# Two-layer graph network on one core: the query and key columns move into the tile of the folded matrices

## The reference

```python
# layer 0
h = relu(layernorm(x));  x = x + adj @ (h @ W0) + b0
# layer 1, 8 heads, n = 128 nodes, dim = 256
h  = relu(layernorm(x))
f  = (h @ fc_w + fc_b)  -> heads x n x 256
q, k = f @ q_w + q_b, f @ k_w + k_b
a  = softmax(leaky_relu(q + k.T + (1 - adj) * -1e9))
x  = x + sigmoid(concat(a @ f) @ fp_w + fp_b + h)
```

## Time and profile before

| | |
|---|---|
| median of 3 runs | 1406.65 us (1406.38 to 1407.17) |
| the profiled execution | 1406.65 us |
| its span, first to last instruction | 1404.9 us |
| granted TensorE clock | 1.0 throughout |
| PE busy | 1394.7 us (99%), 9048 matmuls |
| DVE busy | 1285.1 us (91%) |
| ACT busy | 1126.5 us (80%) |
| POOL busy | 1102.0 us (78%) |

### The profile page before, as it was taken

The page is one execution under the profiler, slowest core; times in us unless marked ns, Lnnn a source line. Parts: engine busy times, 40 slices in busy tenths (PEclk is TensorE's granted clock), DMA queues, the critical chain, the costliest instruction groups (busy, mean ns, idle before and its releaser), DMA issues.

```text
span 1404.9 us, 31603 instructions
## 1 busy us (share of the span) xinstructions
PE 1394.7 (99%) x9048; PEld 1252.5 (89%) x9048; DVE 1285.1 (91%) x4408; ACT 1126.5 (80%) x3429; POOL 1102.0 (78%) x1295
## 2 busy tenths in 40 slices
PE   9999999999999999999999999999999999999998
PEld 7898899899899889998998898998989989988987
DVE  7999999999999999999999999999999999998996
ACT  4878788788888888887888888888878878887876
POOL 4788878878778878778787788787787887888764
PEclk9999999999999999999999999999999999999999
DMA  7423323323223233233232232232332322322221
GB/s 238 98 63 107 107 54 106 91 69 106 71 88 106 55 105 106 54 105 97 63 106 80 79 106 61 99 106 54 105 103 58 106 88 73 106 67 85 77 61 41
DMA packets 177132, 124.69 MB, mean 89 GB/s; under 512 B 137808, under 2 KB 143568, under 8 KB 177104
## 3 DMA queue, kind: packets, MB, share of 16 engines
q1 hardware_dynamic: 176816, 124.35, 30.3%
q10 hardware_dynamic: 288, 0.01, 0.0%
HBM read 105.98 MB, written 18.35 MB: 89 GB/s over the span
## 4 chain that ended last, share of the span: by engine, by line
PE 94%; POOL 2%; issue 1%; DVE 1%; DMA 1%; ACT 0%; POOLq 0%; SPq 0%; ACTq 0%; DVEq 0%
PE gbank L381 48%; PE ybank L381 24%; PE tbank L481 8%; PE bank L381 6%; PE bank L426 4%; PE bank L462 2%; PE bank L449 2%; DMA late<-key_rows 0%; POOL att L1561 0%; POOL att L1554 0%; DMA qk<-qk_w_dram 0%; DVE att L829 0%; POOL xb L1544 0%; POOL t_pos L1546 0%; POOL ends L1577 0%
## 5 line engine op out<-in xcount | busy, mean ns | idle before, releaser
L1233 ACT ACTIVATE att<-att 128x128 f32<-128x128 f32 x1024 | 397.8, 393 | 47.0 <-DVE att L836 44.0
L381 PE MATMUL gbank<-m_hi,hT_lo 128*128 128x512 f32 x1024 | 426.7, 417 | 0.0
L1554 POOL TENSOR_TENSOR att<-late,t_pos 128x512 f32<-128x512 f32 x256 | 330.6, 1293 | 120.5 <-PE tbank L481 115.8
L381 PE MATMUL gbank<-m_hi,hT_hi 128*128 128x512 f32 x1024 | 403.2, 394 | 0.0
L381 PE MATMUL gbank<-m_lo,hT_hi 128*128 128x512 f32 x1024 | 401.3, 392 | 0.0
L812 DVE TENSOR_TENSOR g_lo<-gbank,g_hi 128x512 fp32r<-128x512 f32 x512 | 341.4, 678 | 47.1 <-ACT g_hi L1226 42.0
L1561 POOL TENSOR_TENSOR att<-att,rinv 128x512 f32<-128x512 f32 x256 | 289.4, 1131 | 107.1 <-DVE rinv L841 106.5
L1226 ACT ACTIVATE g_hi<-gbank 128x512 fp32r<-128x512 f32 x512 | 291.1, 595 | 39.6 <-PE gbank L381 39.4
L829 DVE TENSOR_SCALAR_CACHE_REDUCE att<-att,qs 128x128 f32<-128x128 f32 x1024 | 291.6, 341 | 27.0 <-POOL att L1554 26.7
L381 PE MATMUL ybank<-g_hi,pT_hi 128*128 128x256 f32 x1016 | 281.5, 277 | 0.0
L381 PE MATMUL ybank<-g_hi,pT_lo 128*128 128x256 f32 x1016 | 281.4, 277 | 0.0
(11 more groups left out here) (97 smaller groups left out, 2323.1 us busy)
## 6 DMA issues: line engine op xcount, KB each, us to landing
late<-key_rows SPq DMA_DIRECT2D x64, 1024.0 KB, 6.1
g_in<-graph_dram SPq DMA_DIRECT2D x64, 512.0 KB, 3.4
out_dram<-ends SPq DMA_DIRECT2D x63, 256.0 KB, 3.9
qs<-key_rows SPq DMA_DIRECT2D x128, 4.0 KB, 2.5
key_rows<-kq_sb SPq DMA_DIRECT2D x64, 24.0 KB, 1.4
att<-fc_wT_dram SPq DMA_DIRECT2D x4, 256.0 KB, 5.6
late<-fp_w_dram SPq DMA_DIRECT2D x4, 256.0 KB, 5.3
ends<-fp_w_dram SPq DMA_DIRECT2D x2, 512.0 KB, 7.9
```

The source lines that it names most:

```text
L381: mm = pe.matmul(out_ap, w, m, start=first and n == 0, stop=last and n == len(terms) - 1)
L1233: e = act.activation(a[:, s], a[:, s], ACT.Exp, scale=-1.0, bias=a[:, CH + h:CH + h + 1], accum_out=esum[j][c][:, h:h + 1])
L1554: gp.tensor_tensor(a, keys[q][:, j, c * HC:(c + 1) * HC, :], t_pos[q][:, j, :].unsqueeze(1).broadcast_to([P, HC, P]), ALU.add)\
```

## The change

The two query and key columns of each fold no longer go to `u` one fold at a time. They stay next to the matrix they came with, in `m_hi` and `m_lo`, so that one instruction on each of ACT and DVE takes all 258 columns; at the end four small copies on each engine gather all of them into `u`.

- `m_hi` and `m_lo` become `[P, DT, 4, 576]`: for each pair of heads a row of 576 columns, the two matrices at columns 16 to 527, the even head's two extra columns at 14 and 15 and the odd head's at 528 and 529. Their alignment is 256 bytes; a row has 2304 bytes, nine times 256. Each of the two tiles grows from 16384 to 18432 bytes. So the matrices begin at 64 modulo 256, as before. The tiles declared behind begin 4288 bytes later: `g`, `u` and `ident` begin at 0 modulo 256.
- In `fp_sb` the weights lie in rows of 260 columns, with query and key columns on both sides; an even head's fold streams columns 0 to 257, an odd one's 2 to 259. POOL fills both sides in four copies of half the size. PE's `fold` waits for one of them at n = 0, for two at n = 2, for four at n = 8.
- `fold_high` and `fold_low` are one instruction each. `u_high` (ACT, four copies, behind `hT_high(0, 0)`) and `u_low` (DVE, four products with -1, ahead of `hT_low(0, 0)`) are new; the first `queries_keys` waits for these. `u_none` moves from in front of `fold_high(0)` to behind `fold_high(9)`.

```diff
-        m_hi, m_lo = sb("m_hi", [P, DT, H * D], F32R, LINE), sb("m_lo", [P, DT, H * D], F32R, LINE)
+        m_hi, m_lo = sb("m_hi", [P, DT, HP, MROW], F32R, SPAN), sb("m_lo", [P, DT, HP, MROW], F32R, SPAN)
...
+        def u_of(m, dt, k):
+            s = MAT - 2 if k == 0 else MAT + 2 * D
+            return m[:, dt, :, s:s + 2].rearrange("p a k -> p k a").bitcast(F32)
+
+        def fold_at(m, dt, h):
+            s = MAT - 2 if h % 2 == 0 else MAT + D
+            return m[:, dt, h // 2, s:s + D + 2]
...
-                if n == 0:
-                    pe.wait_ge(g_qk, 2)
+                if n in (0, DT, HP * DT):
+                    pe.wait_ge(g_qk, (1, 2, 4)[(0, DT, HP * DT).index(n)])
+                cols = slice(0, D + 2) if h % 2 == 0 else slice(2, D + 4)
...
-                dve.wait_ge(a_uhi, n + 1)
-                dve.scalar_tensor_tensor(out=u_at(dt, h, HALF), in0=gbank[n % RSIZE][:, D:D + 2], scalar=-1.0,
-                                         in1=u_at(dt, h, 0).bitcast(F32), op0=ALU.mult, op1=ALU.subtract)\
-                   .then_inc(v_ulo, 1)
-                s = slice(h * D, (h + 1) * D)
-                dve.tensor_tensor(m_lo[:, dt, s], gbank[n % RSIZE][:, 0:D], m_hi[:, dt, s].bitcast(F32), ALU.subtract).then_inc(v_m, 1)
+                dve.tensor_tensor(fold_at(m_lo, dt, h), gbank[n % RSIZE][:, 0:D + 2], fold_at(m_hi, dt, h).bitcast(F32),
+                                  ALU.subtract).then_inc(v_m, 1)
...
+            def u_low():
+                dve.wait_ge(v_m, H * DT)
+                dve.wait_ge(a_none, 1)
+                for dt in range(DT):
+                    for k in range(2):
+                        dve.tensor_scalar(u_at(dt, HALF, k), u_of(m_lo, dt, k), -1.0, None, ALU.mult).then_inc(v_ulo, 1)
...
                 fold_low(15)
+                u_low()
                 hT_low(0, 0)
...
-                act.activation(m_hi[:, dt, h * D:(h + 1) * D], gbank[n % RSIZE][:, 0:D], ACT.Copy).then_inc(a_m, 1)
-                if n == 0:
-                    act.wait_ge(a_none, 1)
-                act.activation(u_at(dt, h, 0), gbank[n % RSIZE][:, D:D + 2], ACT.Copy, scale=-1.0).then_inc(a_uhi, 1)
+                act.activation(fold_at(m_hi, dt, h), gbank[n % RSIZE][:, 0:D + 2], ACT.Copy).then_inc(a_m, 1)
...
+            def u_high():
+                act.wait_ge(a_m, H * DT)
+                act.wait_ge(a_none, 1)
+                for dt in range(DT):
+                    for k in range(2):
+                        act.activation(u_at(dt, 0, k), u_of(m_hi, dt, k), ACT.Copy, scale=-1.0).then_inc(a_uhi, 1)
...
                 hT_high(0, 0)
+                u_high()
                 h0_relu(2, 2)
...
-                    gp.tensor_copy(w[:, :, D:D + 2].rearrange("p (h t) k -> p h t k", t=DT),
-                                   qk[:].unsqueeze(1).broadcast_to([P, H // 2, DT, 2])).then_inc(g_qk, 1)
+                    for s in (0, 1):
+                        cols = w[:, :, s * (D + 2):s * (D + 2) + 2].rearrange("p (a s t) k -> p a s t k", s=2, t=DT)
+                        gp.tensor_copy(cols[:, :, s], qk[:].unsqueeze(1).broadcast_to([P, HP // 2, DT, 2]))\
+                          .then_inc(g_qk, 1)
```

More of the change, by code:

```diff
@@ L30 @@
 SPAN = 256
+HP = H // 2
+MAT = LINE // 4
+MROW = 2 * D + 64
+FROW = D + 4
 U = 3
@@ L119, in gnn_pair @@
         key_rows = [nc.dram_tensor(f"key_rows{k}", [2 * HALF, P], F32).ap() for k in range(U)]
-        late = sb("late", [P, U * KEYS * P + H * DT])
+        late = sb("late", [P, U * KEYS * P + H * 4])
         keys = [late[:, k * KEYS * P:(k + 1) * KEYS * P].rearrange("p (j h n) -> p j h n", j=J, h=H) for k in range(U)]
@@ L126, in gnn_pair @@
         rinv = [two(f"rinv{j}", [P, HC]) for j in range(J)]
-        ends = sb("ends", [P, 4 * J * D + H * DT])
+        ends = sb("ends", [P, 4 * J * D + H * 4])
         y, th, sg, res = [ends[:, k * J * D:(k + 1) * J * D].rearrange("p (j d) -> p j d", j=J) for k in range(4)]
@@ L135, in gnn_pair @@
         fcT_sb = [w.rearrange("p (t d) -> p t d", d=D) for w in (att_all[:, 0:H * D], late[:, 0:H * D])]
-        fp_sb = [w.rearrange("p (t d) -> p t d", d=D + 2)
+        fp_sb = [w.rearrange("p (t d) -> p t d", d=FROW)
                  for w in (late[:, (U - 1) * KEYS * P:], ends)]
@@ L183, in adjT_of, with u_at @@
             return g_in[q][:, J * D + J * P:].rearrange("p (j n) -> p j n", j=J)
-        def u_at(dt, h, at):
-            return u[:, dt, at:at + ROWS].rearrange("p (k h) -> p h k", k=2)[:, h, :]
+        def u_at(dt, at, k):
+            return u[:, dt, at:at + ROWS].rearrange("p (k a s) -> p k a s", k=2, s=2)[:, :, :, k]
+        def u_of(m, dt, k):
[4 more added lines that the diff above has]
+            return m[:, dt, h // 2, s:s + D + 2]
         def steady(eng, step, first, last):
@@ L217, in weights_out @@
                 at = slice(t.start % H, t.start % H + t.stop - t.start)
-                sp.dma_start(fp_sb[t.start // H][:, at, 0:D], fp_w[:, t, :]).then_inc(s_weights[c], 16)
+                sp.dma_start(fp_sb[t.start // H][:, at, 2:D + 2], fp_w[:, t, :]).then_inc(s_weights[c], 16)
             def load_w0():
@@ L401, in fold @@
                     mm = pe.matmul(gbank[n % RSIZE][:, 0:D + 2], fcT_sb[t // H][:, t % H, dt * P:(dt + 1) * P],
-                                   fp_sb[t // H][:, t % H, :], start=kt == 0, stop=kt == DT - 1)
+                                   fp_sb[t // H][:, t % H, cols], start=kt == 0, stop=kt == DT - 1)
                 mm.then_inc(pe_m, 1)
@@ L456, in queries_keys @@
                 if not has(p - 1):
-                    pe.wait_ge(a_uhi, H * DT)
-                    pe.wait_ge(v_ulo, H * DT)
+                    pe.wait_ge(a_uhi, 2 * DT)
+                    pe.wait_ge(v_ulo, 2 * DT)
                 for dt in range(DT):
@@ L469, in project @@
                     pe.wait_ge(v_m, H * DT)
-                j, s = n // GC, slice(n % GC * BANK, (n % GC + 1) * BANK)
+                j, hp, mat = n // GC, n % GC, slice(MAT, MAT + 2 * D)
                 split(bank[:],
-                      [((hT_hi[q][:, dt, j, :], hT_lo[q][:, dt, j, :]), (m_hi[:, dt, s], m_lo[:, dt, s]))
+                      [((hT_hi[q][:, dt, j, :], hT_lo[q][:, dt, j, :]), (m_hi[:, dt, hp, mat], m_lo[:, dt, hp, mat]))
                        for dt in range(DT)]).then_inc(pe_g[n], 1)
@@ L719, in bias_part @@
                     dve.wait_ge(s_small, 32)
-                    dve.tensor_scalar(c_part[:], fp_sb[t // H][:, t % H, 0:D], fcb[:, t:t + 1], None, ALU.mult).then_inc(v_cpart, 1)
+                    dve.tensor_scalar(c_part[:], fp_sb[t // H][:, t % H, 2:D + 2], fcb[:, t:t + 1], None, ALU.mult).then_inc(v_cpart, 1)
                 else:
                     dve.wait_ge(v_cpart, t)
-                    dve.scalar_tensor_tensor(out=c_part[:], in0=fp_sb[t // H][:, t % H, 0:D], scalar=fcb[:, t:t + 1], in1=c_part[:],
+                    dve.scalar_tensor_tensor(out=c_part[:], in0=fp_sb[t // H][:, t % H, 2:D + 2], scalar=fcb[:, t:t + 1], in1=c_part[:],
                                              op0=ALU.mult, op1=ALU.add).then_inc(v_cpart, 1)
@@ L1269, in begin @@
                 h0_relu(0, 0)
-                u_none()
                 fold_high(0)
@@ L1282, in begin @@
                 fold_high(9)
+                u_none()
                 fold_high(10)
```

## The result

The changed kernel takes 1425.53 us (1425.15 to 1426.06, 4 runs) against 1406.77 us for the kernel before, run beside it. The ratio is 1.0134, with a 95% interval of 1.0116 to 1.0151: slower by 18.8 us. The direction and the place were forecast; the size was not. The forecast was 1419.8 us, with 13.8 us for the loop, and the time lies 3.5 us above the range's upper end of 1422.0. The profiled execution has a span of 1423.7 us, 18.8 more than before.

What follows compares the result with a forecast made beforehand. The matrix engine PE, busy 99% of the span, was taken to bound the kernel through the distance between matmuls. 1406.65 - 0.6 (start) + 13.8 (`attend` in the loop) = 1419.85, rounded 1419.8 us; range 1405.0 to 1422.0.

Steps and rivals of the forecast that it cites:

- at the slow pace they cost 3072 x 4.5 ns = 13.8 us: PE's loop: with `g` at 0, all `attend` matmuls go from 113 to 118 ns, adding 13.8 us; chance 0.38.
- My upper bound of 5.2 ns: `attend` in the loop: most that rounding of the timeline rows allows per matmul, 16 us in all.
- A term put at nothing: `project`: PE's loop: matmuls of `split` into `gbank` stay as before, no time added.
- the 0.6 us of the start: Start of the kernel: gain between 0 and 1.1 us, taken as 0.6, near the shift of VectorE's mean.
- `queries_keys` as the nearest row: Its 117.5 ns, with `hT` streamed from 0, was the ground for expecting `attend` at the slow pace.
- `ident` "left at 0": `ident`, streamed 1280 times, moves from 64 to 0; one nanosecond each would be 1.3 us, counted as 0.
- The rival that the place doesn't matter: Place of `g` has no effect in the loop, only the start's gain remains: 1406.0 us; chance 0.37.
- step 4: Start, GpSimd: four copies 0.14 us apart end near 6.55, hidden before `variance0` at 6.74; if twice as long, 0.4 us later.
- 0.4 to 0.6 forecast: Start, VectorE: reaches `mean1(0, 0)` 0.4 to 0.6 us earlier, from `u_none` and some six subtractions.
- The wait at `aggregate(2, 2)`: Start, PE: the 0.56 us wait for `h0_relu(2, 2)` shrinks; `aggregate(2, 2)` starts at 28.2 to 28.5 instead of 28.75.
- The lucky term: Start: one `bias_part` of 1.53 us, others 475 ns, may escape contention with GpSimd's addition if it starts 0.3 us earlier.
- step 2: Start: four added copies each on ScalarE (0.2 us) and VectorE (0.3, up to 0.4), mostly covered; uncovered 0.4 us before `queries_keys`.

Runs made afterwards that it cites:

- Experiment 1: Kernel before with only `g` moved, from 64 to 0 modulo 256, by padding: 1424.84 us against 1406.74, ratio 1.0135.
- experiment 3: Changed kernel with `g`, `u`, `ident` padded back to 64 and `att` to 96 modulo 256: 1406.18 us against 1407.05 for the kernel before, ratio 0.9995.
- Experiment 5: Kernel before with only `u` and `ident` moved to 0 modulo 256: 1411.13 us, ratio 1.0030.
- experiment 4: Kernel before with only `att` moved, from 96 to 160 modulo 256: 1413.85 us against 1406.85, ratio 1.0049.
- experiment 2: Changed kernel with `g`, `u`, `ident` padded back to 64 modulo 256, which put `att` at 160: 1413.05 us, ratio 1.0045 to the kernel before.
- experiment 6: Kernel before with `pT` and `g` moved together, by 64 bytes: 1420.21 us, ratio 1.0095; second, by 128 bytes: 1416.64 us, ratio 1.0069.

## Why the prediction was wrong in size

**Right: where the change counts.** What the start gave is too small for the runs to tell, and the shift of `g` from 64 to 0 carried nearly everything. Experiment 1 shows it (18.1 us by the shift alone, of 18.8), and experiment 3 closes it (nothing is left once the operands of PE are back).

**The step that failed is the term "at the slow pace they cost 3072 x 4.5 ns = 13.8 us".** I had seen two paces, 113 and 118 ns, in the kernel before and took for granted that a worse place could only mean the second one. With `g` at 0 the loop runs at neither: 119.6 ns in the mean, with single distances from 116 to 124. 3072 x (119.7 - 113.7) = 18.4 us. My upper bound of 5.2 ns was the rounding of the same two rows, so it bounded what I had seen and not what the operand could do; it was 0.8 ns short, and the range with it. It was too tight as rounding, too: 1.13 and 1.18 us are each uncertain by 0.01, so ten distances allow 7 ns, or 21.5 us. And with no gain at the start, 5.2 ns end at 1406.65 + 16 = 1422.65, not at 1422.0. No row of the kernel before shows a distance for `g` and `pT` level, so the honest end of the range was a wider one.

**A term put at nothing: `project`.** I expected the matmuls into `gbank` as before. Over the whole trace they took 2.2 us more, with their operands at their old places modulo 256 (1.6 us in experiment 1, where they didn't move at all). Of the 5.7 us between forecast and result `attend` has 17.4 - 13.8 = 3.6 and `project` these 2.2; the 0.6 us of the start, which can't be seen, and 0.7 less in `queries_keys` about cancel.

**Right for a reason that fell: `queries_keys` as the nearest row.** I read its 117.5 ns as the price of a stream that starts at 0. Experiment 5 left `hT` at 0, moved `u` (and `ident`), and `queries_keys` went to 114.6 ns in the mean. Whether the place of `u` did that or the matmuls ahead of it isn't separated, but the stream's place alone didn't set the 117.5. So the forecast of slower instead of same rested on a row that didn't bear it, and was in part luck; that `g` at 0 is slow was shown only by experiment 1.

**Wrong: `ident` "left at 0".** The transposes that stream it got no slower (108.9 ns against 109.3 in `transpose_p`), but with `u` it cost 4.4 us through the pace of an `attend` and of the `project`s (experiment 5; the two weren't moved one by one). The effects don't add up: `g` alone costs 18.1, `u` and `ident` alone 4.4, both and more together 18.8. In the changed kernel all four `attend`s are past 119 ns already; that a pace which is bad can't be spoilt again would fit, but no run tests it by itself.

**The rival that the place doesn't matter** is refuted by experiment 1. The Trainium skill (TensorE: Matmul & The Clock Gate, section Step-by-step: what each phase is for) says that a load of weights takes no SBUF read bandwidth from the running matmul. No run here measures that share; what the runs do show is that the place even of a tile that is only loaded as weights (`att` in experiment 4) changes the time by 7 us. The rival had 0.37, for that page and for the remark that both paces occur at one place. That remark was true and is half of the mechanism: the pace is a state which PE carries from one group into the next, and with `g` at 64 the fast state exists, with `g` at 0 no `attend` of the trace has it.

**The start, by its steps.** POOL's four copies start 0.14 us apart as forecast, and `variance0` still waited for DVE (0.27 us at 6.88), so step 4 held. DVE's `mean1(0, 0)` came 0.15 us earlier (19.52 for 19.67) and the `mean0` behind it 0.35 (21.71 for 22.06), of 0.4 to 0.6 forecast. The wait at `aggregate(2, 2)` shrank from 0.56 to 0.15 us, but it starts at 28.60 and not between 28.2 and 28.5. The lucky term didn't come: the slow `bias_part` still took 1.23 us (1.53 before), beside GpSimd's addition. In step 2 the size was right and the cover was not: `u_low` holds DVE for 0.31 us, and `hT_low` starts at 27.02 where it had started at 26.75. 0.16 of that came with ScalarE's `hT_high` (26.27 for 26.11), the rest is DVE, which is now late for it.

```profile
26.71 0.47 DVE L766 TENSOR_SCALAR u<-m_lo 128x8 fp32r<-128x8 f32 x4
27.02 0.68 DVE L808 TENSOR_TENSOR hT_lo<-bank,hT_hi 128x512 fp32r<-128x512 f32 x1
```

`queries_keys(0, 0)` is later for it, by 0.26 us, but `aggregate(2, 2)` behind it waits for ScalarE anyway. The first `transpose_p` came 0.15 us earlier in the changed kernel and 0.59 (45.99) in experiment 2, which has the same start; the last section says what lies between them. Whether the change of the start gains anything in the whole, the runs can't tell: the 0.9 us of experiment 3 are inside the interval.

## What to carry to other kernels

On an engine that is full, look at the distance from start to start of its instructions and at where their operands begin, before the instructions that a diff edits: a tile that grows moves everything declared behind it, and here 4288 bytes cost 30 times the 0.6 us that were forecast for the edit. After a change of layout compare the starts of all of PE's operands modulo 256, those of transposes too, and pad them back to where they were; that brought the time to within 0.1% of the old one. When a bound comes from rows of the state you know, say that it doesn't cover states you haven't seen.

## What the runs showed of the hardware

- In these loops a float32r matmul of 256 columns follows the one before at a steady 113.3 ns or at 112.5 to 125 ns, by the starts of the operands modulo 256 and by what ran before, with no wait shown and at the full granted clock. The distances repeat to a nanosecond from pair to pair, in all runs but the second of experiment 6, which has pairs of 21.52 and of 21.65 us. Shifting tiles by a multiple of 256 bytes changed nothing: with the operands back in place, `m` rows at a new stride and everything behind moved by kilobytes, experiment 3 has the kernel before's 113 ns.
- The pace is handed on. With `m` at 0 the matmuls that stream `m` keep their sum, and the `transform` and `attend`s behind them, at their old places, are 4.5 ns slower each. The mechanism inside PE stays open: the runs show which places are good, and not why.
- Moving a tile also moves where ScalarE, VectorE or GpSimd read and write it, and no run separates that from PE's own reads. The pattern speaks for PE: in the changed kernel three of the four `attend`s of a pair, with different work of the other engines beside them, have the same distances, 117.5, 117.5, 120.9, 120.0 and 124.1 ns, twice over behind the first one, and the fourth settles at 120.0 behind its third.
- The first folds ran at half pace in 6 of the 14 profiled executions. The kernel before (first fence) streams its first twelve matmuls in 2.96 us, the changed one (second fence) in 4.45; behind its first distance six are 428 to 432 ns long instead of 216 to 222:

```profile
6.68 2.96 PE L401 MATMUL gbank<-late,att 128*128 128x258 f32 x12
```

```profile
6.84 4.45 PE L417 MATMUL gbank<-late,att 128*128 128x258 f32 x12
```

  The clock column of that stretch reads 1.00 in both, though a distance that doubles fits the lower of the clock's two levels (1.2 GHz); that it was the clock is not shown. It isn't the change's doing: of the three executions with the changed start experiment 2 has 217 ns and the other two about 430, and of the eleven with the old start four have that. It would account for the difference of 0.4 us between the first `transpose_p`s of the changed kernel and of experiment 2, as far as one execution of each can show. Of its 1.4 us, 0.56 was swallowed by the wait for `h_f` at `aggregate(0, 0)` (there in experiment 2, gone in the row at 11.12 of the changed kernel) and 0.4 by the wait for the weights of fold 8.
